# Layer 0: other orders of steps on TensorE, VectorE, ScalarE and GpSimd

## What is computed

```python
def _branch(x, W, gamma, beta):          # for q, k and v
    h = jnp.einsum('bnd,ed->bne', x, W)
    ...                                   # mean and variance over all 4096 rows
    return jax.nn.sigmoid(4.0 * (hn - V_TH))
...
qk = _heads(q * k) * scale
vv = jnp.einsum('bhnd,bhne->bhde', v_h, v_h)
out = jnp.einsum('bhnd,bhde->bhne', qk, vv)     # then @ Wp.T + bp
...
h = x @ Wm + bm
t = h.reshape(bs * L_ * H, HD)
w = jax.nn.softmax(t @ expert_emb, axis=-1)
topw, topi = jax.lax.top_k(w, K)                # K = 2
hmid = jax.nn.gelu(jnp.einsum('td,edi->tei', t, W1) + b1, approximate=False)
eo = jnp.einsum('tei,eio->teo', hmid, W2) + b2
... # the two chosen experts, weighted, then @ Wo + bo
```

## Time and profile before

| | us |
|---|---|
| median of three runs | 1452.81 |
| the runs | 1452.57 to 1458.37 |
| the profiled execution, its own time | 1453.86 |
| its span | 1452.0 |
| TensorE busy | 1385.7 (95% of the span) |
| VectorE busy | 1205.6 (83%) |
| ScalarE busy | 1103.4 (76%) |
| GpSimd busy | 283.7 (20%) |
| granted TensorE clock, mean | 0.988 |

### The profile page before, as it was taken

How to read it: one execution, slowest core, us unless ns; L and a number is a source line. 1 busy time by engine, 2 the same in 40 slices (tenths; PEclk the granted TensorE clock), 3 DMA queues, 4 the chain that set the end, 5 groups by cost and what they waited for, 6 DMA issues and landing times.

```text
span 1452.0 us, 25984 instructions
## 1 busy us (share of the span) xinstructions
PE 1385.7 (95%) x9655; PEld 690.1 (48%) x9689; DVE 1205.6 (83%) x2663; ACT 1103.4 (76%) x2072; POOL 283.7 (20%) x239
## 2 busy tenths in 40 slices
PE   5989999999989998999999999999999999999998
PEld 4653233332237977333343333334443345565796
DVE  7688858574359988999999999988888878999997
ACT  3568889898867741888878988888888886888545
POOL 6212000000023241111111012111111112234542
PEclk8989999999999999999999999999999999999999
DMA  4166656566420001000000000000000000000000
GB/s 111 28 129 176 164 142 148 154 158 132 135 76 1 1 1 44 31 1 1 1 2 1 1 1 1 2 1 1 1 2 1 1 30 1 1 9 8 8 16 22
DMA packets 43629, 63.28 MB, mean 44 GB/s; under 512 B 5360, under 2 KB 25072, under 8 KB 43120
## 3 DMA queue, kind: packets, MB, share of 16 engines
q1 hardware_dynamic: 43504, 61.62, 16.5%
HBM read 54.27 MB, written 7.34 MB: 42 GB/s over the span
## 4 chain that ended last, share of the span: by engine, by line
PE 65%; DVE 18%; DMA 6%; POOL 4%; ACT 3%; issue 3%; SPq 2%; DVEq 0%; ACTq 0%
PE ps L2021 15%; PE ps L2011 12%; PE ps L1990 6%; PE ps L525 6%; PE ps L515 4%; PE ps L2034 4%; DVE p6ac L2548 3%; PE ps L2001 3%; DMA p1GB<-gscr 3%; DMA tscr<-p1tp 1%; POOL WA L2228 1%; PE ps L534 1%; PE ps L2483 1%; DVE X L213 1%; PE ps L448 1%
## 5 line engine op out<-in xcount | busy, mean ns | idle before, releaser
L2130 ACT ACTIVATE p4E<-ps,p4mx,p4sc 128x512 f32<-128x512 f32 x512 | 393.4, 778 | 62.5 <-DVE p4mx L2083 60.5
L2078 DVE TENSOR_REDUCE p4mx<-ps 128x2 f32<-128x1024 f32 x205 | 249.7, 1218 | 29.3 <-PE ps L2011 28.3
L2021 PE MATMUL ps<-p4E,p4vn 128*64 128x512 f32 x1024 | 243.0, 599 | 0.2
L2011 PE MATMUL ps<-p4T 64*128 64x512 f16 x1536 | 199.3, 379 | 3.8 <-ACT p4E L2130 3.5
L2153 POOL TENSOR_TENSOR p4vn<-p4v,p4zs 128x512 f32<-128x512 f32 x64 | 66.8, 1044 | 503.3 <-DVE p4zs L2086 474.5
L657 DVE SCALAR_TENSOR_TENSOR p1Pb<-ps,WB,p1GB 128x512 f32<-128x512 f32 x128 | 95.2, 748 | 67.8 <-PE ps L525 64.2
L752 ACT ACTIVATE p1g<-ps,WB 128x1024 f32<-128x1024 f32 x128 | 135.8, 1118 | 19.5 <-PE ps L515 19.5
L515 PE MATMUL ps<-p1R,p1w1s 128*128 128x512 bf16 x478 | 124.8, 381 | 11.7 <-ACT xT L752 4.5
L2011 PEld LDWEIGHTS ps<-p4T 64*128 64x128 f16 x1536 | 58.2, 94 | 157.1 <-ACT p4E L2130 86.7
L525 PE MATMUL ps<-p1g,WB 128*32 128x512 f32 x512 | 127.1, 608 | 3.6 <-DMA p1GB<-gscr 3.6
L525 PE MATMUL ps<-xn,WB 128*32 128x512 f32 x256 | 126.2, 605 | 0.0
(11 more groups left out here) (374 smaller groups left out, 2603.0 us busy)
## 6 DMA issues: line engine op xcount, KB each, us to landing
p1GB<-gscr SPq DMA_DIRECT2D x128, 256.0 KB
p1R<-tscr SPq DMA_DIRECT2D x64, 128.0 KB, 5.2
tscr<-p1tp SPq DMA_DIRECT2D x24, 128.0 KB, 3.5
WA<-in_w SPq DMA_DIRECT2D x1, 2632.0 KB, 20.4
WB<-in_w SPq DMA_DIRECT2D x1, 2560.0 KB, 9.1
X<-in_x SPq DMA_DIRECT2D x8, 256.0 KB, 5.4
gscr<-p1gT SPq DMA_DIRECT2D x8, 256.0 KB, 5.3
out<-X SPq DMA_DIRECT2D x7, 256.0 KB, 2.3
```

Source lines behind the costliest of these rows:

```text
L2011: y = p.e.matmul(ps[:, banks[hh], :], t[rows, q, 128 * j:128 * j + 128], t[rows, 2 + r, :], start=o == 0, stop=o == 2)
L2021: t = p.e.matmul(ps[64 * hh:64 * hh + 64, self.bank["ctx", n], :], vn[n % 2][:, j, 64 * hh:64 * hh + 64], E[2 * (n % 2) + hh][:, j, :], st ...
L2078: v.e.tensor_reduce(m, ps[:, low:low + 2, :], AX, ALU.max).then_inc(v.own.h, v.one())
L2130: a.e.activation(self.E[2 * i + hh][:, j, :], ps[:, banks[hh], :], ACT.Exp, bias=self.mx[i][:, j, hh:hh + 1], scale=pre.sc[:, 1, 0:1], acc ...
```

## The change

Four strings of the table `ORDER` change, those of TensorE, VectorE, ScalarE and GpSimd. Each has the same letters as before, as many of each, in another order; SyncE's is the same. No instruction is added or removed, apart from where ScalarE switches between activation tables, and there are 17 table loads in the program before and after. The head of each string, of the five lines of which the two long ones consist:

```diff
@@ -235,22 +235,22 @@
         "tensor": (
-            "ababababababababcdefeeegeegheihgijjeeeeeghkieljgemehekhliigjjeeeemgneheinjgoheinejkhlinjnmnnknppnnnppnnnppnnon"
+            "bababaaababebbebcdfeegehgiejeaeahgekihleijgeemehjgieeejhkgeeienjleheegnimkjehenloimgnhnijnjnpnpnnpnnpnnpnnknpn"
...
         "vector": (
-            "ttututtututaauuaatauavauvavwxvyzABACBCDEDEAFBGACFHDIJKAGBBLMCCNOPDQDRSHAIKJBECTUVADWBFCELDAGMBNCOHDPQKFRSGIJXX"
+            "ttututtuutatuauaatauauvwxyzvvABCvDEaaFBAGABCHIDCJEKLBDMACEFANDBGOPCQARFDHBSIJCKTGUBVDHWELCABCMADNKDEXOXPXFQXRS"
...
         "scalar": (
-            "uuuuuuuu112111211211111212113121111243114211444444444444444444444444444444444443444444444444444444444444444444"
+            "uuuuuuuu111211121112113211121114111243114244444444444444444444444444444444444344444444444444444444444444444444"
...
         "gpsimd": (
-            "ttt5ttt6t666t66655555y55EEFFEFEFEEFEFFEFZ"),
+            "tttt6t6t6t6t6665y5E5E5E55E55FEFFFEFFEEZFF"),
```

More of the change, by code:

```diff
@@ L237 @@
         "tensor": (
-            "ababababababababcdefeeegeegheihgijjeeeeeghkieljgemehekhliigjjeeeemgneheinjgoheinejkhlinjnmnnknppnnnppnnnppnnon"
-            "nppnnnqqpnnnpnnppnnnknppnnnlnppnnnmnqqpnnprnnppnnnnppnnnonppnnnqqpnnnpnnppnnnonpnpnnknppnnnqqpnnnpnnppnnnrnppn"
-            "nnlnppnnnmnqqpnnnppnnnpnnppnnnklnnppnnnmnqqpnnprnppnnnnpnpnnonppnnnqqpnnnpnnppnnnonppnnnknppnnnqqpnnnpnnppnnnr"
-            "nppnnnlnppnnnmnqqpnnnppnnnpnnppnnnlnppnnnmnqqpnnprnnppnnnnppnnnonppnnnqqpnnnpnnppnnnonppnnnnppnnnqqpnnnpnnppnn"
@@ L242 @@
-            "nrnppnnnnppnnnqqpnnnpnnppnnnnppnnnnppnnnqqpnnnpnnppnnnrnppnnnnppnnnqqpnnnpnnppnnnnppnnppqqsr"),
+            "bababaaababebbebcdfeegehgiejeaeahgekihleijgeemehjgieeejhkgeeienjleheegnimkjehenloimgnhnijnjnpnpnnpnnpnnpnnknpn"
+            "npnnpnnppnonknnqqpnnnppnlnnpnnpnnpnnmqqpnrpnnnpnnpnnpnnpnnppnnnqqpnnonpknnnppnnnppnnonppnnnqqnnnppnnnppnnrnnpn"
+            "pnnlnnppnmnnnppnnnppnnnqqnnknppnnpnnpnlnnpmnnpqnqpnpnnpnnpnnpnnpnonnppnrnnnppnnnqqnnnppnonnppnknnppnnnqqpnnnpn"
+            "rnnpnppnnlnnpnnmpnnnpqqnnnppnnpnnpnlnnmpnnpnpqqnpnnnpnnpnnppnnrnnpnnpnonnppnnnppnnnqqnnnppnonnppnnpqnnnpqnnnpp"
@@ L243 @@
+            "nnnrnppnnnpnpnnnppnnnqqnnnppnnpnnpnpnnpnnppnnnqqnnnppnnpnnpnnpnnpnnpqnnnpqnnnppnnpnnrpppqqsr"),
         "vector": (
-            "ttututtututaauuaatauavauvavwxvyzABACBCDEDEAFBGACFHDIJKAGBBLMCCNOPDQDRSHAIKJBECTUVADWBFCELDAGMBNCOHDPQKFRSGIJXX"
-            "TUXXVXXWLMNXXEEYFXEXFXXFGEXXFHIXXJKYOXPQXrRSTUXXVLXXMWNOXXPQRSYXTUXVXXZWX0XGXXYXXXXrXXHIXJXKLMNYXXXXXXGHIJXXKY"
-            "OXPQXrRSXTUXVXLXWMNXOXPQRSYXTXUVXXWXXGXXYXXXXrXXHIXJXKLMNYXXXXXXHIXJXKYOXPQXrRSTUXXVLXXMWNOXXPQRSYXTUXVXXWXXXX"
@@ L247 @@
-            "YXXXXrXXXXYXXXXXXXXYXXXXrXXXXYXXXXXXXXYr"),
+            "ttututtuutatuauaatauauvwxyzvvABCvDEaaFBAGABCHIDCJEKLBDMACEFANDBGOPCQARFDHBSIJCKTGUBVDHWELCABCMADNKDEXOXPXFQXRS"
+            "XFGTXUXXVXXWGIEYJXXLXHIMNXFXXKYOXPJrQRXXSTXUVXXLMXNXOPQYXWRSXGTXUXVXXWXXEYXXXXrXXHFXXKIXXEXFXLMNYGXXJXXHXKOPXQ"
+            "YIXRXSTXXUVXLXMWNXOXPQrRXSXTUYVXXWJXXGXXYXXrXXZXHXKXXIYLXXJXXHMKIXXJXYN0OPXQRXSXTXXUrVLXMXNWOXPXQRXSXTUYVXXWXX"
+            "XXYXXrXXXXXXYXXXXXXXXYXXXXXXXYXXXXrXXXYr"),
         "scalar": (
-            "uuuuuuuu112111211211111212113121111243114211444444444444444444444444444444444443444444444444444444444444444444"
@@ L250 @@
-            "44444444444444444444444444444444444344444444444444444444444444444444444444444444444444444444444444434444444444"
+            "uuuuuuuu111211211121112113211121114111243114244444444444444444444444444444444444344444444444444444444444444444"
+            "44444444444444444444444444444444444443444444444444444444444444444444444444444444444444444444444444344444444444"
             "444444444444444444444444444444444444444444444444444444444444444444444444444444444s"),
         "gpsimd": (
-            "ttt5ttt6t666t66655555y55EEFFEFEFEEFEFFEFZ"),
+            "tttt6t6t6t6t6665y5E5E5E55E55FEFFFEFFEEZFF"),
```

## The result

The changed kernel takes 1445.31 us, the median of 20 runs (1437.47 to 1456.84); the kernel before took 1452.75 in 20 runs beside it. The ratio is 0.9951, with a 95% interval of 0.9937 to 0.9965: some 7 us faster, where 1453, no change, was forecast. The time lies inside the range of 1441 to 1465, but a clear gain came where none was forecast.

A forecast was written before the change was run, and what follows sets the result against it. TensorE bounds 176 to 417 us, ScalarE some 13% behind. After comb 28, +3.0 - 0.4 - 22.4 + 14.0 + 5.0 + 2.0 = +1.2; with the start's -0.5, +0.7: forecast 1453 us, range 1441 to 1465.

The forecast's parts named there:

- The bound and the prices: From 176 to 417 us TensorE is the bound; its steps cost mm1 0.43, comb 0.85 to 0.86 us.
- round trips: TensorE's switches between full width and strips, 0.23 us each; 13 more after comb 28 cost 3.0 us.
- The rest of the layer: Layer 0 from comb 28 to comb 127: all terms there sum to +1.2 us.
- The chain's waits: TensorE waits for gates by DMA at combs 36, 52, 68, 84, 100; a 19.5 us chain costs 14.0 us.
- The clock: After comb 28, new TensorE waits of some 3.5 us bring spells at half clock: 2 us, between 0 and 7.5.
- ScalarE: After comb 28, finer alternation and three exps make TensorE wait for gelus: 5 us, between 3 and 9.
- the old waits: TensorE's small waits from comb 28 to comb 127, mostly pairs behind late gelus, all go: -22.4 us.
- The start: Ahead of comb 28: first sigmoid 3 to 4.3 us earlier, mostly given back by VectorE's weight pieces: -0.5 us.
- The second half of that step: Ahead of comb 28: combs 8 and 20 keep 35.4 and 67.7 us from the first copy of gates.
- The start alone moves: Rival: first gates come 4 us earlier, the rest as forecast: 1449 us, within the forecast's range, no own chance.
- the hidden chain: Rival: the gates' DMA chain after comb 28 fits within TensorE's work: -15, 1439 us; chance 0.28 with cases near it.
- The slower side: Rival: the gates' chain takes its full length at the slower clock: +14.4, 1471 us with a late start; chance 0.26.

The follow-up runs named there:

- e4: The changed kernel with SyncE's exchanges, from the third on, two units' gate loads later; 1428.76 us, 0.9840 of the kernel before.
- e8: The kernel before with three of VectorE's four weight pieces moved behind the batch norm's coefficients; 1446.91 us, 0.9971 of the kernel before.
- e12: The changed kernel with VectorE's weight pieces put back where they stood before; 1446.06 us, 0.9953 of the kernel before.
- e15: New order up to comb 28, old order behind it (third join), with SyncE's exchanges two units' gate loads later; 1446.54 us, 0.9969 of the kernel before.
- e6: The kernel before with SyncE's exchanges two units' gate loads later; 1451.26 us, 0.9994 of the kernel before.
- e3: Old order up to comb 28, the changed kernel's order behind it; 1445.85 us, 0.9970 of the kernel before.
- e2: New order up to comb 28, old order behind it, first join; 1455.20 us, 1.0023 of the kernel before.
- e5: New order up to comb 28, old order behind it, second join; 1457.11 us, 1.0037 of the kernel before.
- e9: New order up to comb 28, old order behind it, third join with row steps spread among gatings; 1449.46 us, 0.9995 of the kernel before.

## Why the prediction was wrong

**The bound and the prices** held. Pairs at 1.85, single combs at 1.00, no 2.30; the last pair's wait gone; round trips at the same price (the earlier trace rows and the rows above).

**The rest of the layer**, +1.2, held: 241.6 and 242.1 from comb 28 to 127 against 241.3 and 240.5, which is +1.0 in the mean. Its sum held term by term, if not comb by comb: against the steps' prices, 221.5, the first trace has 20.1 us of waits. The chain's waits, put at 14.0, are 14.2 and 13.3. The combs were the ones named, but single waits were up to 2.5 off both ways, so that the close sum is in part luck (3.3, 3.7, 3.3, 0 and 3.7 forecast; 5.8, 1.7, 3.3, 0.8 and 2.6 in the first trace). The clock, put at 2, cost 3.0: behind the wait at comb 36 the comb, an mm1 and the next comb took 1.93, 0.97 and 1.25, where the same steps took 0.99, 0.54 and 1.00 in e4, which is 1.6 more, and at comb 68 it is 1.4. The granted clock from 197.0 to 199.5 was 0.50, the lower of its two levels, and the matmuls took 1.07 instead of 0.63. For ScalarE, put at 5, there are at most the 2.9 of waits that were neither; I didn't take them apart. e4 shows the chain by experiment: without it the stretch is 14 us shorter. That the old waits went as well follows from the prices, 6 to 7 us of waits being left in e4 against 22.4 before.

**The start**, -0.5, is the step that failed: in the traces comb 28 comes 2.9 and 7.7 us earlier. In the prediction's words, the pieces "come back in a stretch where VectorE is busy for 89%", and so "what is won at the sigmoid is given back with the pieces". I read a share of 33.0 of 37 us from 53 to 90 as full, and left out the ten microseconds ahead of it, in which VectorE is busy for 2.5. All engines from 38 to 90 us, before and after (VectorE is the third):

```profile
38.00:90.00 52.00, 45.39 (x225) 30.92 (x226) 38.60 (x99) 33.32 (x42) 9.25 (x9) 0.92 0.34 54
```

```profile
38.00:90.00 52.00, 50.25 (x264) 34.22 (x264) 47.80 (x119) 37.93 (x46) 10.90 (x10) 0.95 0.35 61
```

Before, it had 13.4 us idle there (38.60 busy of 52), and nearly 8 of them between the last coefficient at 42.7 and 53, where it waits for the first sigmoids to come back from ScalarE and TensorE:

```profile
45.58 0.69 DVE L601 TENSOR_TENSOR WA<-WA 128x512 f32<-128x512 f32 x1 [2.86 <-ACT WA L732]
49.27 0.29 DVE L593 TENSOR_TENSOR WA<-ps,cst 128x128 f32<-128x128 f32 x1 [2.99 <-PE ps L462]
```

The new order puts the pieces into that gap:

```profile
38.24 0.68 DVE L389 CAST p1R<-p1R 128x1024 bf16<-128x1024 f32 x1
...
40.61 1.28 DVE L396 SCALAR_TENSOR_TENSOR p1w1s<-p1R,cst,p1w1s 128x1024 bf16<-128x1024 bf16 x1
```

They also got shorter there: L396 took 1.28, in the earlier trace rows 2.00, and the five operations that I had put at 6 take 4.9. e8, which moves nothing but these pieces, shows the step wrong by itself: its first copy of gates came 2.2 to 3.4 us earlier. From the first sigmoid to the first copy of gates it is 47.0 and 47.2 us after, 46.9 and 44.6 before: what was won at the sigmoid was kept in the first pair of traces, and two thirds of it in the second. The copy came at 85.4 and 83.7, outside the 88 to 91 that I had named as the test of this term.

The second half of that step failed as well: "both keep their distance from the first copy, 35.4 and 67.7, so long as the transfers set it". To comb 8 it is 36.4 and 29.8 after, 35.4 and 34.3 before. The transfers do set it, and so it varies with what they meet.

**The rivals.** "The start alone moves", 1449, was the mechanism, with 4 us as its bound where the traces have 3 to 8. I had it inside the forecast's range and gave it no chance of its own. The measured 1445.3 falls just under the 1445.5 below which I had put the 0.28 of the hidden chain, but the chain did not hide: that the time came out there, and within the range, speaks for nothing that I had argued. The slower side didn't come: the chain took its full length only at comb 36 of the first trace.

**What stays open.** By the traces the start gives 6.7 us in the mean with a large scatter, and the median moved by 7.4; the two agree, but two traces of the changed kernel can't say more. How the start's gain is shared between the pieces and the earlier mm1 isn't settled (e8 4 to 5 us alone, e12 not told apart from the changed kernel). Nor is why the old rest keeps only some 4 us of it: of the 6.2 by which comb 28 is earlier in e15 than in e6, 3.3 go before comb 127 and 1.7 behind it. The part behind comb 127, nearly all of it other layers, took 1032.9 to 1036.8 us over all traces, and I don't know why.

## What to carry to other kernels

A busy share says how full a stretch is, not whether a given piece of work finds room: before saying that moved work comes back, look at the engine's idle gaps at the place it moves to, beginning where the move takes effect and not some microseconds later. When an order is tightened on the computing engines, read the DMA queue's order again with it: here the new order alone was worth 0.5%, the same order with six exchanges moved two loads down 1.6%, and that same edit nothing on the old order. And when a part is undone by joining two orders, look at the waits at the join before believing the time: two of the three joins that had the new start cost more than the effect they were to measure.

## What the runs showed that I had not expected

- A weight load of 2632 KB issued just ahead of two gate loads of 256 KB held these up: the gates of unit 4 took 14.6 to 21.6 us from issue to landing in the chains of waits of nine traces, gate loads from 120 us on mostly 8 to 10 and at most 13.9 (comb 8 at 110.0 to 112.5 with the load elsewhere, 113.5 to 121.8 with it).
- The changed kernel scatters more than the old one: its runs have a standard deviation of 4.4 and 4.5 us (10 and 20 runs), the old kernel's 1.7 to 3.6 in the jobs here. It isn't the new start as such, nor the weight load alone: e3, with the old start, has 4.4 in 10 runs, while e2, e5 and e15, with the new start ahead of the old rest, have 1.5 to 2.1 (e9 3.8); with the load cut and moved it is 3.9 to 4.6, with the later exchanges alone 2.7 and 1.4 (4 or 5 runs each). The cause is open.
- A VectorE operation (L396, 128x1024) took 2.00 us at 31 us and 1.28 at 41 us. Over all 18 traces it took 1.99 or 2.00 in the six in which GpSimd was at an operation of its own for at least part of it, and 1.28 or 1.29 in the twelve in which GpSimd was idle. No run tests whether that is the reason, and another operation (L400) took 1.28 in e6 beside a busy GpSimd, as it did in all traces without.
